# AdaLN feed-forward on one core: the first product of twelve batches in three single-pass products over exact 12-bit parts, and all projection tiles direct

## The reference

```
q_emb = relu(cond @ W3 + b3)                          # 16 x 512
xs    = (256 * x + sum over tokens of x) * q_emb      # per batch
h     = relu(xs @ W2 + b2)                            # first product, 4096 x 512 x 512
h_q   = 0.5 where h > 0.33, else 0                    # (h is never negative)
w     = 0.6 where weight > 0.2, -0.6 where < -0.2, else 0;  w = w + rram
out   = x + h_q @ w.T                                 # projection, 4096 x 512 x 512
```

## Time and profile before

| | |
|---|---|
| median of three runs | 173.54 us (172.73 to 173.70) |
| profiled execution, span from first to last instruction | 171.1 us; no other time of it is listed |
| TensorE busy | 165.2 us, 97% |
| VectorE busy | 131.6 us, 77% |
| GpSimd busy | 85.4 us, 50% |
| ScalarE busy | 67.7 us, 40% |
| data moved | 28.99 MB |

### The profile page before, as it was taken

How to read it: one execution, slowest core, us unless ns; L and a number is a source line. 1 busy time by engine, 2 the same in 40 slices (tenths; PEclk the granted TensorE clock), 3 DMA queues, 4 the chain that set the end, 5 groups by cost and what they waited for, 6 DMA issues and landing times.

```text
span 171.1 us, 2177 instructions
## 1 busy us (share of the span) xinstructions
PE 165.2 (97%) x684; PEld 122.3 (71%) x684; DVE 131.6 (77%) x196; ACT 67.7 (40%) x173; POOL 85.4 (50%) x85
## 2 busy tenths in 40 slices
PE   7989999999899999999999999999999999999991
PEld 2889997777445478687645459997644459999991
DVE  3589997998999997785978878779926167776751
ACT  2154269927202269998109994531000001001000
POOL 3000950659105691560199002758498003999990
PEclk9999999999999999999999999999999999999999
DMA  5999999999700594609949204993293000353166
GB/s 168 223 238 247 234 217 225 219 222 211 137 0 0 129 356 126 124 9 226 377 173 337 107 0 119 329 347 131 82 325 145 0 4 3 121 199 113 66 255 231
DMA packets 31211, 28.99 MB, mean 169 GB/s; under 512 B 1600, under 2 KB 22368, under 8 KB 31200
## 3 DMA queue, kind: packets, MB, share of 16 engines
q1 hardware_dynamic: 30128, 28.07, 60.4%
q10 hardware_dynamic: 1008, 0.79, 1.6%
q0 software_dynamic: 64, 0.00, 0.0%
HBM read 20.47 MB, written 8.39 MB: 169 GB/s over the span
## 4 chain that ended last, share of the span: by engine, by line
PE 92%; issue 1%; DVE 1%; ACT 0%; ACTq 0%
PE out_ps L955 12%; PE hid_ps L955 10%; PE out_ps L932 9%; PE out_ps L1018 8%; PE hid_ps L925 6%; PE hid_ps L883 6%; PE hid_ps L859 6%; PE hid_ps L898 6%; PE hid_ps L906 6%; PE hid_ps L918 6%; PE hid_ps L866 6%; PE hid_ps L1005 5%; PE hid_ps L1010 4%; PE hid_ps L932 2%; ACT xT L430 0%
## 5 line engine op out<-in xcount | busy, mean ns | idle before, releaser
L430 ACT ACTIVATE xT<-xT,coef,q_scale 128x256 f32<-128x256 f32 x64 | 33.9, 592 | 14.0 <-DVE coef L583 7.8
L532 DVE STREAM_TRANSPOSE xT<-x_in 128x1024 f32<-128x1024 f32 x15 | 30.8, 2060 | 0.1
L436 ACT ACTIVATE junk<-xT,q_emb 128x256 bf16<-128x256 f32 x40 | 19.8, 496 | 11.6 <-DVE xT L532 11.4
L370 POOL TENSOR_TENSOR x_res<-x_res,pieces 128x256 f32<-128x256 f32 x8 | 5.9, 734 | 27.3 <-DVE x_res L706 27.3
L486 ACT ACTIVATE pieces<-out_ps 128x256 f32<-128x256 f32 x6 | 2.3, 387 | 32.5 <-PE out_ps L955 29.6
L1018 PE MATMUL out_ps<-xT,w_sb 128*128 128x512 f32 x32 | 14.1, 600 | 0.0
L376 POOL TENSOR_TENSOR x_res<-x_res,pieces 128x256 f32<-128x256 f32 x16 | 13.5, 863 | 0.0
L932 PE MATMUL out_ps<-wT_lo,hid 128*128 128x512 f32 x32 | 13.3, 415 | 0.0
L932 PE MATMUL out_ps<-wT_hi,hid 128*128 128x512 f32 x32 | 12.5, 390 | 0.0
L1018 PEld LDWEIGHTS out_ps<-xT,w_sb 128*128 128x128 f32 x32 | 9.8, 309 | 3.7
L883 PE MATMUL hid_ps<-t_sum,s_mix 128*128 128x512 f32 x24 | 11.4, 595 | 0.7 <-issue 0.7
(11 more groups left out here) (134 smaller groups left out, 415.8 us busy)
## 6 DMA issues: line engine op xcount, KB each, us to landing
x_in<-in_x SPq DMA_DIRECT2D x24, 256.0 KB, 5.4
x_res<-in_x SPq DMA_DIRECT2D x3, 2048.0 KB, 9.2
out<-x_res SPq DMA_DIRECT2D x24, 256.0 KB, 3.6
x_in<-in_x SPq DMA_DIRECT2D x1, 2048.0 KB, 9.8
out<-x_in SPq DMA_DIRECT2D x7, 256.0 KB, 2.1
x_in<-in_x SPq DMA_DIRECT2D x12, 128.0 KB, 6.5
w_sb<-in_L_cond_W SPq DMA_DIRECT2D x4, 256.0 KB, 6.4
x_res<-in_L_ffn_weight SPq DMA_DIRECT2D x4, 256.0 KB, 7.1
```

The costliest lines, as they stand in the source:

```text
L430: nc.scalar.activation(part, part, ACT.Identity, bias=coef[:, n, k:k + 1], scale=q_scale[:, n, k:k + 1]).then_inc(s_xs, 1)
L532: nc.vector.transpose(xT[:, s, :, cols].rearrange("p j (n t) -> p n j t", t=BLK), x_in[:, p % SLOTS, b * NB:(b + 1) * NB].rearrange("p n ( ...
```

## The change: three passes over exact parts, direct tiles, new orders

Strassen goes, in both products, and with it the sums of tokens, of w2, of hidden values and of projection weights. Batches are handled in blocks of two (8 blocks of 512 tokens, 4 tiles each). Blocks 0 and 1 stay direct in four-byte floats. For blocks 2 to 7:

- Scaled x and w2 are each split into a high part (written as fp32r, ScalarE, after a factor 1 - 2^-13) and the exact rest (GpSimd). A third operand is made of each: the high part times (1 + 1/4096) minus x on VectorE (`difference`), and high/4096 minus rest of w2 on GpSimd.
- `multiply(b)`: for each of 4 column chunks m, three passes of 4 matmuls (k) with 512 columns, fp32r: high x high and low x low into one bank (main), difference x difference into another (cross). The parts of w2 are stored with the columns of a chunk adjacent (`columns_of`).
- ScalarE turns cross into a bound (`bound_of`), VectorE compares main with it (`compare`) into `hid`. Two pairs of banks alternate: the unit u (block and chunk) waits until unit u-2 is compared.
- All 32 projection tiles are direct (`project`), the last in two halves as before. The order on TensorE is multiply(2), multiply(3), project(0), project(1), then multiply(b), project(b-2) for b = 4 to 7, and the rest.
- `hid` holds four blocks, `xT` three. Residuals are loaded in eight pieces of 1 MB. The token sums of batches 3, 5, 10, 12 and 14 are on VectorE, of 2, 4, 6 to 9, 11, 13 and 15 on ScalarE. The second half of `wT_lo` is made on VectorE. The zeroed warm-up tile has 1024 two-byte columns instead of 512.

```diff
-    VECTOR_SUMS = (2, 3, 6, 7)
+    VECTOR_SUMS = (3, 5, 10, 12, 14)
...
-        warm = sbuf("warm", [P, D], mybir.dt.bfloat16)
+        warm = sbuf("warm", [P, 2 * D], mybir.dt.bfloat16)
...
@@ SyncE
+            sp.wait_ge(s_wT, 2)
+            load_res(0)
+            sp.wait_ge(s_wsum, 4)
+            load_res(1)
+            sp.wait_ge(s_tr, 9)
+            load_pair(6)
+            store(0)
+            sp.wait_ge(s_tr, 11)
+            load_pair(7)
+            for b in range(1, BLOCKS):
+                if b < BLOCKS - 2:
+                    sp.wait_ge(s_stored[b - 1], DMA * TILES)
+                    load_res(b + 1)
...
@@ GpSimd
+            def low_part(n):
+                pool.wait_ge(s_xk_h, n - FIRST + 1)
+                for k in range(0, KD, 2):
+                    ks = slice(k, k + 2)
+                    nc.gpsimd.tensor_tensor(part_of(xk_l, n)[:, ks], batch_of(n)[:, ks],
+                                            part_of(xk_h, n)[:, ks].bitcast(F32), ALU.subtract).then_inc(s_xk_l, 1)
...
+            for k in range(KD):
+                pool.wait_ge(s_w2_round, k + 1)
+                nc.gpsimd.tensor_tensor(columns_of(wk_l, k), by_columns(w2_sb[:, k]),
+                                        by_columns(w2_round_sb[:, k].bitcast(F32)), ALU.subtract).then_inc(s_wk_l, 1)
+            for k in range(KD):
+                pool.wait_ge(s_wk_h, k + 1)
+                pool.wait_ge(s_wk_l, k + 1)
+                nc.gpsimd.tensor_tensor(columns_of(wk_d, k), columns_of(wk_h, k).bitcast(F32),
+                                        columns_of(wk_l, k).bitcast(F32), ALU.subtract).then_inc(s_wk_d, 1)
+            low_part(4)
+            low_part(5)
+            low_part(6)
+            for i in range(3):
+                quantize_weight(i)
+            low_part(7)
+            quantize_weight(3)
+            for i in range(4):
+                sum_weight(i)
+            weight_low(0)
+            for n in range(8, B):
+                low_part(n)
...
@@ ScalarE
+            def high_part(n):
+                act.wait_ge(s_xs, XS_DONE[n])
+                if n >= FIRST + 4:
+                    act.wait_ge(s_main, KD * (n // 2 - DIRECT - 1))
+                nc.scalar.activation(part_of(xk_h, n), batch_of(n), ACT.Copy, scale=SHRINK).then_inc(s_xk_h, 1)
...
+            def bound_of(b, m):
+                u = KD * (b - DIRECT) + m
+                act.wait_ge(s_th, 1)
+                act.wait_ge(s_cross, u + 1)
+                if u >= 2:
+                    act.wait_ge(s_hid, u - 1)
+                nc.scalar.activation(bound[:, u % 2], hid_ps[2 * (u % 2)][:], ACT.Identity, bias=th_col[:, m:m + 1],
+                                     scale=CUT).then_inc(s_bound, 1)
...
+            accumulate(4)
+            scale(4)
+            high_part(4)
+            scale(5)
+            high_part(5)
+            accumulate(6)
+            scale(6)
+            high_part(6)
+            bound_of(2, 0)
+            accumulate(7)
+            scale(7, (0, 1))
+            bound_of(2, 1)
+            scale(7, (2, 3))
+            high_part(7)
+            bound_of(2, 2)
+            bound_of(2, 3)
+            bound_of(3, 0)
+            weight_high(0)
+            bound_of(3, 1)
+            weight_high(1)
...
@@ VectorE
+            def difference(n):
+                dve.wait_ge(s_xk_h, n - FIRST + 1)
+                if n < FIRST + 2:
+                    dve.wait_ge(s_wk_h, KD)
+                    dve.wait_ge(s_wk_l, KD)
+                for k in range(0, KD, 2):
+                    ks = slice(k, k + 2)
+                    nc.vector.scalar_tensor_tensor(part_of(xk_d, n)[:, ks], part_of(xk_h, n)[:, ks].bitcast(F32),
+                                                   1.0 + 1.0 / CUT, batch_of(n)[:, ks],
+                                                   ALU.mult, ALU.subtract).then_inc(s_xk_d, 1)
...
+            def compare(b, m):
+                u = KD * (b - DIRECT) + m
+                dve.wait_ge(s_main, u + 1)
+                dve.wait_ge(s_bound, u + 1)
+                if b >= 4:
+                    dve.wait_ge(s_out_ps, TILES * (b - 3))
+                nc.vector.scalar_tensor_tensor(hid[:, b % 4, m], hid_ps[2 * (u % 2) + 1][:], CUT + 1.0, bound[:, u % 2],
+                                               ALU.mult, ALU.is_gt).then_inc(s_hid, 1)
...
+            transpose_batch(5)
+            sum_batch(5)
+            compare_weight()
+            transpose_batch(6)
+            difference(4)
+            difference(5)
+            quantize(0, 0)
+            quantize(0, 1)
+            transpose_batch(7)
+            quantize(0, 2)
+            quantize(0, 3)
+            difference(6)
+            compare(2, 0)
+            compare(2, 1)
+            quantize(1, 0)
+            difference(7)
+            compare(2, 2)
+            quantize(1, 1)
+            quantize(1, 2)
+            compare(2, 3)
+            quantize(1, 3)
+            compare(3, 0)
+            transpose_weight(0)
+            transpose_weight(1)
+            compare(3, 1)
+            weight_low(1)
+            transpose_batch(8)
+            compare(3, 2)
+            compare(3, 3)
+            transpose_batch(9)
+            finish(0, 0)
+            finish(0, 1)
+            difference(8)
+            finish(0, 2)
+            finish(0, 3)
+            transpose_batch(10)
+            finish(1, 0)
+            difference(9)
+            finish(1, 1)
+            sum_batch(10)
+            finish(1, 2)
+            finish(1, 3)
+            transpose_batch(11)
+            for b in range(4, BLOCKS):
+                n = 2 * (b + 1)
+                compare(b, 0)
+                if n < B:
+                    difference(n)
+                compare(b, 1)
+                if n + 2 < B:
+                    transpose_batch(n + 2)
+                compare(b, 2)
+                if n < B:
+                    difference(n + 1)
+                compare(b, 3)
+                finish(b - 2, 0)
+                if n + 2 < B:
+                    sum_batch(n + 2)
+                finish(b - 2, 1)
+                finish(b - 2, 2)
+                finish(b - 2, 3)
+                if n + 2 < B:
+                    transpose_batch(n + 3)
...
@@ TensorE
+            def multiply(b):
+                for m in range(KD):
+                    u = KD * (b - DIRECT) + m
+                    cross, main = hid_ps[2 * (u % 2)], hid_ps[2 * (u % 2) + 1]
+                    if u == 0:
+                        pe.wait_ge(s_wk_d, KD)
+                    if u < 2:
+                        pe.wait_ge(s_cls_hid, 2 * u + 2)
+                    else:
+                        pe.wait_ge(s_hid, u - 1)
+                    pe.wait_ge(s_xk_h, 2 * (b - DIRECT + 1))
+                    for k in range(KD):
+                        nc.tensor.matmul(main[:], wk_h[:, m, k], xk_h[:, b % 2, k], start=(k == 0), stop=False)
+                    pe.wait_ge(s_xk_d, 4 * (b - DIRECT + 1))
+                    for k in range(KD):
+                        mm = nc.tensor.matmul(cross[:], wk_d[:, m, k], xk_d[:, b % 2, k],
+                                              start=(k == 0), stop=(k == KD - 1))
+                    mm.then_inc(s_cross, 1)
+                    pe.wait_ge(s_xk_l, 4 * (b - DIRECT + 1))
+                    for k in range(KD):
+                        mm = nc.tensor.matmul(main[:], wk_l[:, m, k], xk_l[:, b % 2, k], start=False, stop=(k == KD - 1))
+                    mm.then_inc(s_main, 1)
...
+            multiply(2)
+            multiply(3)
+            project(0)
+            project(1)
+            for b in range(4, BLOCKS):
+                multiply(b)
+                project(b - 2)
+            project(BLOCKS - 2)
+            project(BLOCKS - 1, range(TILES - 1))
+            for h, cols in enumerate(COLS):
+                project_part(BLOCKS - 1, TILES - 1, hid_ps[h], cols)
```

More of the change, by code:

```diff
@@ L154, in adaln_ffn_kernel @@
         s_x_in = [sem(f"x_in_loaded{p}") for p in range(PAIRS)]
[L155 to L156 removed]
+        s_x_res = [sem(f"x_res_loaded{b}") for b in range(BLOCKS)]
+        s_stored = [sem(f"stored{b}") for b in range(BLOCKS)]
         s_cond = sem("cond_loaded")
@@ L212, in adaln_ffn_kernel @@
         s_whi = sem("weight_hi_ready")
-        s_wlo = sem("weight_lo_ready")
+        s_wlo = [sem(f"weight_lo_ready{h}") for h in range(2)]
         def load_first(engine, half, quads):
@@ L520, in _ @@
+            for h in range(2):
+                act.wait_ge(s_out, LAST + 1 + h)
+                act.dma_start(out_tiles[LAST, :, COLS[h]], res(LAST)[:, COLS[h]]).then_inc(s_stored[BLOCKS - 1], DMA)
         @block.vector
@@ L829, in _ @@
             for _ in range(WARM):
-                nc.tensor.matmul(out_ps[3][:], warm[:, 0:P], warm[:], start=True, stop=True)
+                nc.tensor.matmul(out_ps[3][:], warm[:, 0:P], warm[:, 0:D], start=True, stop=True)
             pe.wait_ge(s_condT, QUADS)
@@ L951, in pair_product @@
```

(30 more changed lines are left out.)

776 lines of the change are left out of this document (164 added, 612 removed).

## The result

The changed kernel takes 175.76 us (median of four executions, 174.8 to 176.34), the kernel before 173.62 in the same rounds: the ratio is 1.015, with a 95% interval of 1.010 to 1.020. It is slower, where 171.5 us and faster were predicted; the time lies above the range. The profiled execution spans 172.8 us, against 171.1 before and 169.1 by the sum.

The account below looks back on a forecast made before the run. TensorE, busy 97% of the span, was taken as the bound. First product -6.6, projection +3.1, old stalls -1.3 (-4.9 before rounding), start +0.2, new waits +2.7 gave -2.0: span 169.1, time 171.5 us, range 169.3 to 174.6.

Parts of the forecast that it names:

- First product: Blocks 2 to 7 on TensorE: 288 single-pass matmuls at 0.2275 us replace three Strassen groups of 72.1 us; -6.6 us.
- Projection: Second product on TensorE: eleven tile pairs go direct, 3.64 us a pair instead of Strassen's 3.36; +3.1 us.
- Old stalls: TensorE's waits and hand-overs in Strassen's chain, 1.3 us of the old stretch, all go; -1.3 us.
- What difference really costs: VectorE's differences contend with GpSimd's low parts: 2.4 us a pair instead of 1.2; stalls put at +2.7 us.
- the walk: Engine queues followed in code order with 2.4 us per difference: TensorE stalls of 3.0 us in sum.
- Start: Kernel start: doubled warm-up tile delays it, +0.2 us; ScalarE's and GpSimd's new w2 work there costs 0.
- later than 39.2: Sign that the prediction is wrong: the direct products of batches 0 to 3 end after 39.2 us.
- New waits, blocks 2 and 3: Queues walked at 1.2 us per difference: block 2 starts at 38.86 with 1.4 us to spare; stalls 0.9 us.
- the second walk: Queues walked again at 2.4: delays at quantization (0,3), units 4 and 7, compares of units 8 and 9; 3.0 us.
- rival C: VectorE yields wholly to low_part, 3.8 us per difference; block 2 starts 1.0 late; 174.0 us; chance 0.18.
- D: Rival: VectorE becomes the bound in later blocks, 18.4 us a block against TensorE's 18.2; 176.6 to 179.2 us; chance 0.12.
- fair share: VectorE's difference beside GpSimd's low part, the two sharing: 1.75 us per difference, stalls 2.2 us in sum.

Follow-up runs that it names:

- The first: Changed kernel, with GpSimd's w2 subtractions waiting until VectorE has finished the chunk coefficients of batches 0 and 1: 174.23 us, ratio 0.995 to the kernel before.
- the fourth experiment: Changed kernel, with each of GpSimd's four 512-element w2 subtractions cut into four of 128 at the same place: 174.81 us, ratio 0.997 to the kernel before.
- e3_both: Changed kernel, with w2 subtractions held until the chunk coefficients are done and each low part until its difference is done: 173.83 us, ratio 0.996 to the kernel before.
- e7_quantize_again: Changed kernel, with w2 subtractions delayed and two quantizations ahead of transpose 6 and the differences, second run: 172.01 us, ratio 0.992 to the kernel before.
- e8_unit7: Changed kernel, w2 subtractions delayed, two quantizations first, compare(3,1) ahead of transpose_weight(1), bound_of(3,1) ahead of weight_high(0): 171.77 us, ratio 0.992 to the kernel before.

## Why the prediction was wrong

**The terms on TensorE were right.** "First product": 65.5 us predicted, 24 x 2.72 = 65.3 measured; weight loads with adjacent columns took 188 ns, below the spacing of 227. "Projection": 56.4 predicted for 31 tiles, 56.2 measured. "Old stalls": the Strassen hand-overs are gone. TensorE's work is 123.4 us for the 123.9 of the sum, which is the predicted -4.9 and 0.5 more.

**"What difference really costs" had the right size.** 2.4 us was taken for a pair beside a low part; 2.39 was measured (73.44), 5.13 for the four of batches 4 and 5. In part that was luck: 2.4 was a choice between two rows, not worked out from what the two engines do to each other, which is told in the last section. The units lose 3.3 us in sum by their starts (1.18 at units 1 to 3, 1.06 at unit 7, 1.02 at units 10 and 11: what stands between two starts beyond 2.72 us), 3.4 with rounding, where 2.7 was taken and the walk gave 3.0. The walk had 1.3 at unit 7 and 1.25 at units 10 and 11, close to the measured; it had 0.3 before unit 1 and 0.2 at unit 4, which does not wait.

**The step that failed is "Start"**, in its sentence on GpSimd's eight w2 subtractions: "Not needed before 38.9". It asked when their result is needed and not whom they hold up while they run. The earlier trace rows gave the price for a large instruction (2.28 for 1.23 us), and it was applied to the differences alone. The chunk-wise start is a ring of small instructions with no slack: two held by 1.06 and 1.77 us cost the direct products 1.4 us at their end (40.23 instead of 38.86), against +0.2 in the sum; the prediction's own sign of being wrong, "later than 39.2", came true. Transpose 6 starts 3.3 us late (34.76 instead of the planned 31.5), its load's wait included. The first and the fourth experiment show the cause. Not all of the 3.3 us are its doing: with the subtractions delayed, transpose 6 still starts at 32.91, because the weight compare is held instead and the load costs 0.41 us.

**"New waits, blocks 2 and 3" then failed at "block 2 starts at 38.86 with 1.4 us to spare".** There the differences of 4 and 5 were walked at 1.2 us a pair. Two pairs at 2.4 end the quantizations at 37.4 + 2.4 = 39.8, 0.9 us after the 38.86, but the second walk's list has no delay at block 2's start; its 0.3 at quantization (0,3) fits only one of the two pairs stretched. Only rival C has block 2 late, by 1.0. In the profile both are stretched (5.13 us for the four) and transpose 6 is 3.3 late, so the quantizations ended at 43.2: TensorE idles 3.1 us. The experiments on the order show that this wait goes when the two quantizations stand ahead.

**By the profile the difference closes.** Start +1.2 over the sum, block 2's start +3.1, the units +0.7 (3.4 less 2.7), the work on TensorE -0.5 (123.4 against 123.9), and the tail behind the last matmul 2.65 instead of 3.45 us, -0.8: 3.7 us, which is 172.8 - 169.1. The median misses by 4.26; the 0.5 more fits the clock, since the profiled execution had it full and half of the timed ones didn't.

**The clock was not among the rivals.** The sum holds the full clock everywhere because every slice of the earlier trace rows shows it. A wait of 3 us can change that: behind it the granted clock goes to half, 1.2 GHz, for a while. In the profiles it did so behind waits of 2.25, 2.76, 2.85, 3.06, 3.12 and 3.60 us; behind one of 2.24 and one of 3.08 it did not, nor, after the chunk-wise start, behind any of 1.53 or less. The mean was below full in six of the changed kernel's eight executions and in all four of the kernel before with the added wait, and it costs 1.3 us (176.3 against 175.0 in the first rounds) to 1.7 us (the eight records, 5.34 for 3.60). But the mean does not tell the place: three profiles (e3_both, e7_quantize_again, e8_unit7) have the granted clock near half from 11 to 13 us, where TensorE had waited no more than 0.6 us just before. The Trainium skill, "TensorE: Matmul & The Clock Gate", Part 1, says that the array returns to half rate after an idle stretch; these runs agree, behind 2.25 to 3.60 us of idle time, but not always: the profile after has 3.08 us and the full clock. Nor does that sentence cover the three profiles with the half clock from 11 to 13 us. Had block 2's wait been seen, the sum would have had 1.3 to 1.7 us more for the executions that lose the clock.

**Rivals.** D came nearest in time and was wrong in mechanism: in later blocks VectorE keeps up, and from 101.14 us nothing makes TensorE wait. What made the kernel slower was at the start, before the first of the new matmuls.

## What to carry to other kernels

Work moved to GpSimd early, into a time when "nothing needs it", is not free: ask which small VectorE instructions it will run beside (with two SBUF inputs above all, but a TENSOR_SCALAR was held here too), and whether they lie in a chain without slack. Put instructions that free what TensorE wants next (here two quantizations) ahead of preparations that it wants later, and move the lists of all engines that feed a step, not of one. By this kernel's rows, price a new wait of TensorE of 3 us as 3 us and, in most executions, 1.3 to 1.7 us of halved clock behind it.

## What the runs showed of the hardware

**A VectorE instruction is held whole, not slowed.** A 128x1 or 128x16 instruction ended with the GpSimd instruction that was running (11.97, 14.05), pieces of 0.63 us held it for at most about one piece (0.71 us in all), and twice it was let in at none of the boundaries between GpSimd's instructions that it met, but when GpSimd paused (5.41 us in the execution of 177.25 us, 1.76 in one of 172.03). Transposes and reductions, with one SBUF input, kept their 2.05 and 0.42 us beside GpSimd's work; the 128x16 TENSOR_SCALAR, which has one input too, was held. The Trainium skill, "SBUF — State Buffer", section "Who interferes with whom", says that the pair of ports goes to whoever issues first, for a whole instruction, and that the other is fully blocked; it names two SBUF inputs and the two-port modes, which TENSOR_SCALAR can enter. The small rows agree (1.22 and 1.95 us). So does the pair at 73.44, by its sum: 2.39 us is the first difference, 0.68, the second, as long, and about 1 us for an instruction of the low part between them. The 5.41 and the 1.76 do not: read literally, the waiting instruction would have run at GpSimd's next boundary, within 2.1 and 1.3 us. For the "fair share" of 1.75 us these profiles show no support: the pair took 2.39.

**Strided reads.** ScalarE needs 1.13 us for 128x512 whose elements are four apart, 0.62 for adjacent ones; GpSimd 2.13 against 1.28. Both are about what the prediction allowed ("perhaps double" 0.55, and 2.3).

**Not shown:** why the clock falls in some executions of the changed kernel and not in others, what lowers it at 11 to 13 us in three profiles, and what lets a small instruction in at a boundary in one execution and not in another.
